# Two graph layers in one software pipeline: the second layer's mask moves from TensorE's products to GpSimd, with all lists and banks laid out anew

## The chip, the cores and the metric

The kernel runs on one core of a Trainium2 chip. The metric is the device time of one execution in microseconds, median of three runs. A core has TensorE (PE in the profile; PEld is its weight load), VectorE (DVE), ScalarE (ACT), GpSimd (POOL) and SyncE (SP), which here only issues DMAs. All share SBUF; PSUM has eight banks, each 128 partitions by 512 f32.

## The reference

64 graphs of 256 nodes with 256 features; `adj` has 0 and 1. Eight heads of width 32.

```
# layer 0
q, k = src@Wq+bq, src@Wk+bk;  attn = softmax(q k^T / sqrt(32))       # per head
out = sum over r of (attn * (adj == r)) @ (src@Wv[r] + bv[r])        # r = 0..3
x  = LN(src + out@Wo + bo);   x2 = LN(x + gelu(x@W1+b1)@W2 + b2)
# layer 1
e  = leaky_relu(q k^T, 0.2);  attn = softmax(where(adj > 0, e, -9e15))
h  = LN(attn @ v)
y  = LN(concat(h, x2) @ Wffn^T) + x2
```

Layer 0's softmax runs over all nodes, and the relations are sorted out afterwards; layer 1's runs over the neighbours alone, and it is this mask (`adj > 0`) that the change moves.

## The kernel before

One graph is worked on by four stages, and each engine's `body(g0, g1, g2, g3)` holds one period of its list: four neighbouring graphs, each in another stage, with g3 the youngest. `turns` runs the body 67 times: three partly filled at the start, a hardware loop, three partly empty at the end. The order of each list is written out by hand; semaphores (`sig`) tie them. Banks are assigned by number (`B_Q`, `B_RR`, ...), and many waits only say that a bank or a tile is free again.

Products that need f32 accuracy are made of three f32r products of high and low parts. So after most results comes a split: a cast to f32r (high part), then a subtraction (low part): `low` on GpSimd (L418, for act, att and xt) and `lo_part`, `biased_low` on VectorE (L719, L804). Scores are computed from stacks (`stack_a`, `stack_r`), in which SP's DMAs put high and low parts of one head under one another, three DMAs per pair of heads.

Per graph, on TensorE: stage g3 is layer 0's projections (`projection`, `vee`), score rows for the maxima (`score_rows`, L1103), their turning (`maxima_turned`), score columns (`score_cols`, L1112), and values (`both` for sums and relation 0, `one` for relation 1 minus 0, L1024). Stage g2 is out projection, FFN (`up`, `down`) and layer 1's projections. Stage g1 is layer 1's attention and FFN.

Layer 1's attention goes by four pairs of heads. `masked_rows(p, b)` (L1034 to L1041) writes 2 x 256 x 256 scores and adds `off_q` (bf16, 0 or -9e15) by an identity matrix; then ScalarE's `low` copies 0.2 times the scores to `leaky_s` (L534), VectorE's `leaky` takes the maximum of both (L790), `lowest_row` reduces the row maximum (L794), ScalarE's `exp_rows` (L540) applies exp in place with the row sums, TensorE's `turn` (L1048) transposes, ScalarE copies to `probs`, and `row_values` multiplies with v. `leaky_s` has three slots for four pairs.

GpSimd's other work: `masked(p)` (L424) multiplies layer 0's exp with `rel1` (adj == 1) in pairs of 128x512; `make_rstd` (L412, L414) for the four layer norms LN_A, LN_M (layer 0), LN_H, LN_O (layer 1); `residual` (L430). VectorE's `centre` (L740) and `rescale` (L746) are the norms' two passes, each in two halves. `rel1` is made on VectorE at L829, `off_q` at L850, and L856 checks adj_a. In the list before, GpSimd waits for LN_H's rescale before its second `masked`:

```
if g0 is not None:
    pool.wait_ge(ln_mv[LN_H].sem, ln_mv[LN_H].at(g0))
    make_rstd(LN_H, g0)
    pool.wait_ge(ln_done[LN_H].sem, ln_done[LN_H].at(g0))
```

Of the kernel before, what the change touches and what calls it, by code (L numbers as in the profile page):

```python
# [29 lines left out]
P = 128  # L30
# [78 lines left out]
def build(nc, x, xT, adj, adjT, w):  # L109
    ctx = ExitStack()  # L110
    with ctx:
# [32 lines left out]
        identb = sb("identb", [P, P], BF16)  # L144
# [55 lines left out]
        def bank(b):  # L200
            return pair[b // 2][:, b % 2]

        B_AO, B_ADEN, B_Q, B_K, B_WO, B_X1T, B_RV, B_HN = 2, 6, 7, 6, 1, 4, 4, 2
        B_DN, B_N1T, B_FFN, B_AMT, B_X2T, B_LQ, B_LK, B_LV = 1, 1, 3, 4, 1, 4, 7, 7
        B_X = 0
        B_V, B_UP = (5, 7), (4, 6, 1, 5)
        B_RR, B_TN, B_AR, B_AC = (0, 2, 1, 0), (0, 1, 1, 3), (3, 1, 2, 3), (2, 3, 2, 0)
# [31 lines left out]
                                                   sig("low_r_done", PAIRS))  # L239
        exp_r_done, turned_mm, probs_r = sig("exp_r_done", PAIRS), sig("turned_mm", PAIRS), sig("probs_r", PAIRS)  # L240
# [49 lines left out]
        def _(sp):  # L290
# [29 lines left out]
            def body(g0, g1, g2, g3):  # L320
                if g2 is not None:
                    load(xn, x, g2, "(t p) c -> p t c", ld_xn)
                if g3 is not None:
                    load(xt, xT, g3, "(t p) n -> p t n", ld_xt)
                if g2 is not None:
                    sp.wait_ge(ashift.sem, ashift.at(g2))
                    for s in range(2):
                        sp.dma_start(stack_a[STK + s:STK + s + 1, 0, :, :].bitcast(F32),
                                     shift_a[32 * s:32 * s + H, :].bitcast(F32)).then_inc(ashifted.sem, 16)
                    if path.general:  # L330
                        load_x_terms(g2)
                if g1 is not None:
# [4 lines left out]
                    stack(3, stack_r, stacked_r)  # L337
                if g2 is not None:
                    load(adj_q, adj, g2, "(t p) n -> p t n", ld_adj_r)
                if g3 is not None:  # L340
                    sp.wait_ge(qk_split.sem, qk_split.at(g3))
                    stack(0, stack_a, stacked_a)
                    stack(1, stack_a, stacked_a)
                    stack(2, stack_a, stacked_a)
                    stack(3, stack_a, stacked_a)
                    load(adj_a, adjT, g3, "(t p) n -> p t n", ld_adj_a)
                if g0 is not None:
                    sp.wait_ge(ln_done[LN_O].sem, ln_done[LN_O].at(g0))
                    sp.dma_start(out[g0 - path.general * G].rearrange("(t p) c -> p t c", p=P), result[:]).then_inc(stored.sem, 16)

# [46 lines left out]
        def _(pool):  # L397
# [28 lines left out]

            def residual():
# [18 lines left out]
            def body(g0, g1, g2, g3):  # L446
                if g1 is not None:
                    pool.wait_ge(att_hi_done.sem, att_hi_done.at(g1))
                    low(att_lo[:], att[:], att_hi[:]).then_inc(att_split.sem, 1)
                    pool.wait_ge(ln_mv[LN_A].sem, ln_mv[LN_A].at(g1))  # L450
                    make_rstd(LN_A, g1)
                    pool.wait_ge(act_hi_done.sem, act_hi_done.at(g1, 1))
                    low(act_lo[:, 0], act[:, 0], act_hi[:, 0]).then_inc(act_split.sem, 1)
                    pool.wait_ge(act_hi_done.sem, act_hi_done.at(g1, 2))
                    low(act_lo[:, 1], act[:, 1], act_hi[:, 1]).then_inc(act_split.sem, 1)
                    pool.wait_ge(act_hi_done.sem, act_hi_done.at(g1, 3))
                    low(act_lo[:, 2], act[:, 2], act_hi[:, 2]).then_inc(act_split.sem, 1)
                    pool.wait_ge(act_hi_done.sem, act_hi_done.at(g1))
                    low(act_lo[:, 0], act[:, 0], act_hi[:, 0]).then_inc(act_split.sem, 1)
# [3 lines left out]
                if g0 is not None:  # L463
                    pool.wait_ge(ln_done[LN_M].sem, ln_done[LN_M].at(g0))
                    if ran(g0, 1):
                        pool.wait_ge(ln_done[LN_O].sem, ln_done[LN_O].at(g0 - 1))
                    residual().then_inc(x2k_done.sem, 1)
                if g1 is not None:
                    pool.wait_ge(ln_mv[LN_M].sem, ln_mv[LN_M].at(g1))
                    make_rstd(LN_M, g1)  # L470
                if g2 is not None:
                    pool.wait_ge(probs_a.sem, probs_a.at(g2, 1))
                    pool.wait_ge(rel1_done.sem, rel1_done.at(g2))
                    masked(0).then_inc(probs1_done.sem, 1)
# [33 lines left out]
        def _(act_e):  # L508
# [862 lines left out]
```

## Time and profile before

| | before |
|---|---|
| time, median of 3 runs (lowest, highest) | 3195.21 us (3192.64, 3196.96) |
| the profiled execution's span | 3190.8 us |
| TensorE busy | 3103.2 us (97%) |
| VectorE busy | 2604.6 us (82%) |
| ScalarE busy | 2056.7 us (64%) |
| GpSimd busy | 1432.6 us (45%) |
| mean granted TensorE clock | 0.989 |

The profile gives the profiled execution's time as the span from its first to its last instruction; there is no other time of that execution. A steady period is one graph. TensorE's durations overlap each other, since a product starts before the last one has drained; its cost is read from the distance between starts. On VectorE, too, a next independent instruction starts about 0.09 us before the end of the last.

### The profile page before, as it was taken

Reading aid. Unit: us, or ns where it says so; the run is one execution under the profiler, and the core shown is the slowest. Engines: PE = TensorE matmul, PEld = TensorE weight load, DVE = VectorE, ACT = ScalarE, POOL = GpSimd, SP = SyncE. Lnnn points to the kernel's source line nnn. Section 1 sums busy time; section 2 is a strip of 40 time slices with the busy share of each in tenths; the row PEclk is TensorE's granted clock in tenths of the full one; section 3 lists DMA queues with packets and bytes.
Section 4 is the critical chain, followed back from the end, with each engine's and each line's share of the span. In section 5 each row is a group of like instructions: output and inputs, shape, how many; then the busy total and the mean of one; then the engine's idle time right before and its main releaser. Section 6 shows DMA issues by size and latency. Waiting matters only on the chain.

```text
span 3190.8 us, 76499 instructions
## 1 busy us (share of the span) xinstructions
PE 3103.2 (97%) x28139; PEld 2715.8 (85%) x28328; DVE 2604.6 (82%) x4896; ACT 2056.7 (64%) x4303; POOL 1432.6 (45%) x1549
## 2 busy tenths in 40 slices
PE   5999999999999999999999999999999999999996
PEld 4888888888888888888888888888888888888885
DVE  4788888888888888888888888888888888888884
ACT  2565766766766766766766766766766766666664
POOL 1445445445445445445445445445344444444441
PEclk8999999999999999999999999999999999999997
DMA  4343344344334334434434434433433433433431
GB/s 111 84 101 93 89 94 97 89 92 98 91 89 98 94 86 98 96 83 98 99 81 98 102 79 97 105 79 94 107 79 92 110 79 89 112 80 89 107 81 31
DMA packets 218074, 292.76 MB, mean 92 GB/s; under 512 B 31796, under 2 KB 119479, under 8 KB 218039
## 3 DMA queue, kind: packets, MB, share of 16 engines
q1 hardware_dynamic: 218038, 292.30, 39.0%
q8 instruction: 22, 0.36, 0.0%
q14 instruction: 14, 0.11, 0.0%
HBM read 73.02 MB, written 16.78 MB: 28 GB/s over the span
## 4 chain that ended last, share of the span: by engine, by line
PE 90%; ACT 3%; issue 3%; DVE 2%; SPq 1%; DMA 1%; POOL 0%; POOLq 0%; DVEq 0%; ACTq 0%
PE pair L994 50%; PE pair L1024 15%; PE pair L1048 7%; PE pair L1038 6%; PE pair L1103 4%; PE pair L1112 2%; PE pair L1040 2%; ACT probs L561 2%; PE pair L1012 2%; SPq L299 1%; PE pair L999 1%; PE pair L1119 0%; ACT leaky_s L540 0%; DMA stack_a<-qk 0%; DMA probs<-in_w 0%
## 5 line engine op out<-in xcount | busy, mean ns | idle before, releaser
L418 POOL TENSOR_TENSOR act_r_lo<-act,act_r_hi 128x512 fp32r<-128x512 f32 x256 | 335.3, 1319 | 741.6 <-DVE act_r_hi L931 537.5
L540 ACT ACTIVATE leaky_s<-leaky_s,low_r 128x256 f32<-128x256 f32 x1024 | 506.1, 499 | 2.7 <-DVE low_r L794 2.0
L424 POOL TENSOR_TENSOR probs<-probs,rel 128x512 f32<-128x512 f32 x256 | 293.4, 1168 | 207.0 <-ACT probs L561 119.8
L561 ACT ACTIVATE probs<-pair 128x1024 f32<-128x1024 f32 x256 | 256.8, 1029 | 189.9 <-PE pair L1112 189.9
L798 DVE TENSOR_REDUCE mx_a<-pair 128x4 f32<-128x1024 f32 x256 | 307.7, 1223 | 78.1 <-PE pair L1103 78.0
L534 ACT ACTIVATE leaky_s<-pair 128x1024 f32<-128x1024 f32 x256 | 262.6, 1026 | 158.7 <-PE pair L1040 158.7
L790 DVE TENSOR_TENSOR leaky_s<-pair,leaky_s 128x1024 f32<-128x1024 f32 x256 | 312.4, 1220 | 37.8 <-ACT leaky_s L534 37.5
L794 DVE TENSOR_REDUCE low_r<-leaky_s 128x4 f32<-128x1024 f32 x256 | 310.8, 1214 | 2.2
L530 ACT ACTIVATE probs<-pair 128x1024 f32<-128x1024 f32 x256 | 261.8, 1023 | 65.1 <-PE pair L1048 60.9
L424 POOL TENSOR_TENSOR leaky_s<-probs,rel 128x512 f32<-128x512 f32 x256 | 291.0, 1173 | 0.2 <-ACT probs L561 0.2
L1048 PE MATMUL pair<-ident,leaky_s 128*128 128x128 f32 x2048 | 269.7, 275 | 6.7 <-ACT leaky_s L540 5.8
L555 ACT ACTIVATE act<-pair,bias_col 128x256 f32<-128x256 f32 x512 | 215.8, 476 | 76.4 <-PE pair L994 75.0
L1048 PEld LDWEIGHTS pair<-ident,leaky_s 128*128 128x128 f32 x2048 | 237.0, 142 | 18.5 <-ACT leaky_s L540 7.5
L412 POOL TENSOR_TENSOR rstd<-mv,eps 128x2 f32<-128x2 f32 x256 | 73.0, 285 | 398.4 <-DVE mv L735 398.4
L1038 PE MATMUL pair<-stack_r 96*128 96x256 f32 x1024 | 242.3, 348 | 4.6 <-DMA stack_r<-qk 3.2
L874 DVE RECIPROCAL att<-pair 128x512 f32<-128x512 f32 x64 | 214.9, 3358 | 36.6 <-PE pair L1024 36.6
L1024 PE MATMUL pair<-probs,v_a 128*32 128x256 f32 x3072 | 207.0, 387 | 11.7 <-ACT probs L561 11.6
L1038 PEld LDWEIGHTS pair<-stack_r 96*128 96x128 f32 x1024 | 179.2, 194 | 42.2 <-issue 25.9
L994 PE MATMUL pair<-xt_r_hi,w_hi 128*128 128x256 f32 x1024 | 211.3, 287 | 1.4 <-DVE xt_r_lo L719 1.4
L530 ACT ACTIVATE v_r<-pair 128x512 f32<-128x512 f32 x64 | 38.2, 597 | 269.8 <-PE pair L994 269.8
L994 PE MATMUL pair<-w_hi,act_r_hi 128*128 128x256 f32 x1024 | 209.9, 286 | 0.0
L994 PE MATMUL pair<-xt_r_hi,w_lo 128*128 128x256 f32 x1024 | 206.2, 283 | 0.0
(193 smaller groups left out, 8839.7 us busy)
## 6 DMA issues: line engine op xcount, KB each, us to landing
stack_a<-qk SPq DMA_DIRECT2D x768, 128.0 KB, 2.5
stack_r<-qk SPq DMA_DIRECT2D x768, 128.0 KB, 2.4
xt<-in_xT SPq DMA_DIRECT2D x64, 256.0 KB, 3.4
adj_a<-in_adjT SPq DMA_DIRECT2D x64, 256.0 KB, 3.0
xn<-in_x SPq DMA_DIRECT2D x64, 256.0 KB, 3.2
adj_q<-in_adj SPq DMA_DIRECT2D x64, 256.0 KB, 2.9
out<-n SPq DMA_DIRECT2D x64, 256.0 KB, 2.8
probs<-in_w SPq DMA_DIRECT2D x4, 512.0 KB, 4.6
```

What stands on the lines that cost most here:

```text
L418: return nc.gpsimd.tensor_tensor(dst, src, hi, ALU.subtract)
L424: last = nc.gpsimd.tensor_tensor(masked_p[g][:, h], probs[:, g, h], rel1[:], ALU.mult)
L530: return nc.scalar.activation(dst, src, ACT.Copy)
L540: last = nc.scalar.activation(leaky_s[:, p % SLOTS, k, t], leaky_s[:, p % SLOTS, k, t], ACT.Exp, bias=low_r[:, p, k, t:t + 1], accum_out=d ...
L561: return nc.scalar.activation(probs[:, g, 2 * q:2 * q + 2], pair[b][:], ACT.Exp, scale=SCALE)
L790: return nc.vector.tensor_tensor(leaky_s[:, p % SLOTS], pair[b][:], leaky_s[:, p % SLOTS], ALU.max)
L794: return nc.vector.tensor_reduce(low_r[:, p], leaky_s[:, p % SLOTS], AX.X, ALU.max, negate=True)
L798: return nc.vector.tensor_reduce(mx_a[:, :, p * NG:(p + 1) * NG].rearrange("p t h -> p h t"), pair[b][:], AX.X, ALU.max)
L994: last = mm(dst, lhs(i, t), rhs(j, t), start=start and n == 0, stop=stop and n == len(steps) - 1, skip_group_check=skip)
L1024: last = mm(bank(b)[h * DH:(h + 1) * DH, g, :], v(t, g * GH + h), pr(h, t), start=first and t == 0, stop=stop and t == NT - 1, skip_group_ ...
L1038: mm(pair[b][:, k, t], stack_r[:, 0, slot(h), t * P:(t + 1) * P], stack_r[:, 1, slot(h), :], start=t == 0, stop=False, skip_group_check=True)
L1048: last = nc.tensor.transpose(pair[b][:, k, c, t * P:(t + 1) * P], leaky_s[:, p % SLOTS, k, t, c * P:(c + 1) * P], ident[:])
```

## The change

The mask of layer 1 goes. In its place GpSimd adds `off_q` in place to `leaky_s`, between `leaky` and `lowest_row`, under a new signal `masked_r`. `identb` and the identity products are gone. All five lists and all bank numbers are new, and with them the waits on banks. The core of it:

```diff
-        identb = sb("identb", [P, P], BF16)
-        B_AO, B_ADEN, B_Q, B_K, B_WO, B_X1T, B_RV, B_HN = 2, 6, 7, 6, 1, 4, 4, 2
-        B_DN, B_N1T, B_FFN, B_AMT, B_X2T, B_LQ, B_LK, B_LV = 1, 1, 3, 4, 1, 4, 7, 7
+        B_AO, B_ADEN, B_Q, B_K, B_WO, B_X1T, B_RV, B_HN = 3, 2, 4, 2, 3, 0, 3, 0
+        B_N1T, B_DN, B_FFN, B_AMT, B_X2T, B_LQ, B_LK, B_LV = 4, 0, 5, 1, 1, 7, 0, 5
-        B_V, B_UP = (5, 7), (4, 6, 1, 5)
-        B_RR, B_TN, B_AR, B_AC = (0, 2, 1, 0), (0, 1, 1, 3), (3, 1, 2, 3), (2, 3, 2, 0)
+        B_V, B_UP = (3, 1), (1, 7, 0, 1)
+        B_RR, B_TN, B_AR, B_AC = (3, 0, 3, 1), (2, 2, 3, 1), (1, 3, 2, 1), (3, 0, 1, 3)
+        masked_r = sig("masked_r", PAIRS)
...
+            def without_edges(p):
+                for k in range(2):
+                    last = nc.gpsimd.tensor_tensor(leaky_s[:, p % SLOTS, k], leaky_s[:, p % SLOTS, k], off_q[:], ALU.add)
+                return last
...
-            def masked_rows(p, b):
+            def second_rows(p, b):
                 for k, h in enumerate((p, p + GH)):
                     for t in range(NT):
-                        mm(pair[b][:, k, t], stack_r[:, 0, slot(h), t * P:(t + 1) * P], stack_r[:, 1, slot(h), :],
-                           start=t == 0, stop=False, skip_group_check=True)
-                    last = mm(pair[b][:, k], identb[:], off_q[:], start=False, stop=True, skip_group_check=True)
+                        last = mm(pair[b][:, k, t], stack_r[:, 0, slot(h), t * P:(t + 1) * P], stack_r[:, 1, slot(h), :],
+                                  start=t == 0, stop=True, skip_group_check=True)
```

The new lists, one period each, in words ("A(g3)" is A for the youngest graph; waits for data left out):

- SP: xt(g3); the shift's two DMAs(g2); adj_a(g3), which waits for the check of the graph before; stack_r 0, 1, 2(g1); adj_q(g2); stack_r 3(g1); stack_a 1, 0, 2, 3(g3); store(g0); xn(g3). Before, xn and xt stood first, adj_q behind stack_r 3, and adj_a behind stack_a, in the order 0, 1, 2, 3.
- GpSimd: low part of xt(g3), low part of att(g2), edges 0, edges 1(g1), rstd LN_A(g2), rstd LN_O(g0), edges 2, edges 3(g1), low part of act 0(g2), residual(g1), low parts of act 1, 2, 3(g2), rstd LN_M(g2), masked 0, 1(g3), rstd LN_H(g1), masked 2, 3(g3). "Edges" is `without_edges`.
- ScalarE: exp_cols 0, 1, 2(g2), x2t(g1), exp_cols 3(g2), the two copies of layer 1's q and k(g1), n1t(g0), low 0, 1, 2(g1), biased q, k(g3), v_r(g1), exp_rows 0(g1), v_a 0, 1(g3), x1t(g2), exp_rows 1, low 3, copy of turned 0(g1), gelu 0, 1, 2(g2), copy 1(g1), gelu 3(g2), exp_rows 2, 3, copies 2, 3, copy of the values(g1).
- VectorE: cast of xt(g3); reciprocal, minimum of the check, attention multiply, cast of att(g2); LN_O statistics(g0); leaky 0(g1); LN_O centre(g0); leaky 1(g1); residual and LN_A statistics(g2); lowest_row 0(g1); LN_A centre(g2); biased_low q(g3); LN_A rescale(g2); lowest_row 1(g1); biased_low k(g3); low part of x1t(g2); leaky 2(g1); LN_O rescale(g0); leaky 3, lowest_row 2(g1); cast of act 0(g2); rel1(g3); cast of act 1(g2); lowest_row 3(g1); cast of act 2(g2); maxima 0 to 3(g3); cast of act 3(g2); shift(g3); rden(g1); residual, LN_M statistics, centre, rescale, off_q(g2); per_head(g1); low part of x2t(g2); LN_H statistics, centre, rescale(g1); check of adj_a(g3); qk_lo 0, 1(g2); low part of n1t(g1).
- TensorE: wq(g3), rows 1(g1), out projection(g2), rows 2(g1), wk(g3), lv(g1), vee 0, 1(g3), x1t(g2), turn 0, rows 3(g1), up 0, 1, 2(g2), turn 1(g1), up 3(g2), score_rows 0, 1, 2(g3), down 0(g2), score_rows 3(g3), down 1(g2), turn 2(g1), turned maxima(g3), down 2(g2), turn 3(g1), down 3(g2), row values(g1), score_cols 0, 1(g3), FFN's x2t half(g1), score_cols 2(g3), turned values(g1), x2t(g2), score_cols 3, both 0(g3), lq, lk(g2), n1t(g1), both 1(g3), FFN's other half(g1), one 0, 1(g3), rows 0(g2). "Rows" is `second_rows`. Before, lv stood behind the FFN's half, and turn 1 before up 0.

## Rows read from the trace of the kernel before

**Rows 1.** The page: span; busy time of each engine, share, instructions.
```profile
span 3190.8 us, 76499 instructions
PE 3103.2 (97%) x28139; PEld 2715.8 (85%) x28328; DVE 2604.6 (82%) x4896; ACT 2056.7 (64%) x4303; POOL 1432.6 (45%) x1549
```
**Rows 2.** The page: the chain that ended last, by engine.
```profile
PE 90%; ACT 3%; issue 3%; DVE 2%; SPq 1%; DMA 1%; POOL 0%; POOLq 0%; DVEq 0%; ACTq 0%
```
**Rows 3.** VectorE's line 874: durations in ns, first and last start in us.
```profile
L874 DVE RECIPROCAL att<-pair x64: 3357/3358/3359, 68.4 to 3096.7; 128x512 f32<-128x512 f32 x64
```
**Rows 4.** One steady period: length; busy PE, PEld, DVE, ACT, POOL; clock, DMA, GB/s.
```profile
1502.30:1550.39 48.09, 47.92 (x439) 42.10 (x443) 40.28 (x77) 31.94 (x68) 22.34 (x25) 1.00 0.40 93
```
**Rows 5.** Timeline of TensorE, merged: start, us to the last one's end.
```profile
1518.43 0.87 PE L1038 MATMUL pair<-stack_r 96*128 96x256 f32 x4
...
1519.61 0.41 PE L994 MATMUL pair<-wo_lo,att_r_hi 128*128 128x256 f32 x2
...
1528.87 0.40 PE L994 MATMUL pair<-xt_r_lo,w_hi 128*128 128x256 f32 x2
...
1538.90 0.71 PE L1103 MATMUL pair<-stack_a 96*128 96x256 f32 x4
1539.44 0.40 PE L994 MATMUL pair<-w_hi,act_r_hi 128*128 128x256 f32 x2
...
1541.74 0.38 PE L1119 MATMUL pair<-ident,mx_a 128*8 128x128 f32 x2
...
1546.21 0.50 PE L994 MATMUL pair<-wf_hi,x2t_hi 128*128 128x256 f32 x2
```
**Rows 6.** Timeline of GpSimd: four mask multiplies in a row.
```profile
1508.66 4.54 POOL L424 TENSOR_TENSOR leaky_s<-probs,rel 128x512 f32<-128x512 f32 x4
```
**Rows 7.** Timeline of VectorE in the same period.
```profile
1510.14 3.36 DVE L874 RECIPROCAL att<-pair 128x512 f32<-128x512 f32 x1 [0.41 <-PE pair L1024]
...
1516.41 0.68 DVE L886 TENSOR_TENSOR att<-pair,att 128x512 f32<-128x512 f32 x1
1517.13 0.43 DVE L888 CAST att_r_hi<-att 128x512 fp32r<-128x512 f32 x1
1517.47 1.21 DVE L794 TENSOR_REDUCE low_r<-leaky_s 128x4 f32<-128x1024 f32 x1
1518.60 1.22 DVE L790 TENSOR_TENSOR leaky_s<-pair,leaky_s 128x1024 f32<-128x1024 f32 x1
...
1522.03 0.75 DVE L731 BATCH_NORM_STATS2 stats<-res 128x6 f32<-128x256 f32 x2
...
1523.04 0.84 DVE L804 SCALAR_TENSOR_TENSOR qk<-pair,bias_col,qk 128x256 fp32r<-128x256 f32 x2
1523.80 0.87 DVE L740 SCALAR_TENSOR_TENSOR x<-res,mv,norm 128x256 f32<-128x256 f32 x2
```
**Rows 8.** Timeline early on: VectorE's check, the GpSimd multiplies; the check's group.
```profile
106.39 1.65 DVE L856 SCALAR_TENSOR_TENSOR adj_a<-adj_a,rel 128x512 int32<-128x512 int32 x1
...
106.14 1.35 POOL L424 TENSOR_TENSOR probs<-probs,rel 128x512 f32<-128x512 f32 x1
...
107.45 1.62 POOL L424 TENSOR_TENSOR leaky_s<-probs,rel 128x512 f32<-128x512 f32 x1
...
L856 DVE SCALAR_TENSOR_TENSOR adj_a<-adj_a,rel 128x512 int32<-128x512 int32 x64 | 45.4, 709 | 0.0
```
**Rows 9.** Timeline: a cast of act beside GpSimd's subtraction.
```profile
1533.57 0.61 DVE L937 CAST act_r_hi<-act 128x512 fp32r<-128x512 f32 x1
...
1532.60 1.29 POOL L418 TENSOR_TENSOR act_r_lo<-act,act_r_hi 128x512 fp32r<-128x512 f32 x1 [8.43 <-DVE act_r_hi L931]
```
**Rows 10.** Waits of GpSimd: in total, times, longest.
```profile
POOL probs L424 <- DVE n L746: 87.2, 62, 1.4
```
**Rows 11.** While draining: a gap of TensorE, then the clock (columns as rows 4).
```profile
3111.49 0.66 PE L1012 MATMUL pair<-ident,x 128*128 128x128 f32 x4 [2.12 <-DVE x L746]
...
3112.90:3116.20 3.30, 3.30 (x18) 3.30 (x18) 2.62 (x3) 2.31 (x2) 0.00 (x0) 0.53 0.00 0
```

More of the change, by code:

```diff
@@ L446, in body @@
             def body(g0, g1, g2, g3):
[L447 to L459, printed above, removed]
                 if g3 is not None:
@@ L854, in body @@
-                if g2 is not None and not path.general:
-                    dve.wait_ge(rel1_done.sem, rel1_done.at(g2))
-                    nc.vector.scalar_tensor_tensor(adj_a[:], adj_a[:], 0, rel1[:], ALU.is_equal, ALU.add,
-                                                   accum_out=known[:]).then_inc(known_done.sem, 1)
-                if g0 is not None:
-                    dve.wait_ge(ln_mid[LN_H].sem, ln_mid[LN_H].at(g0))
-                    dve.wait_ge(ln_rstd[LN_H].sem, ln_rstd[LN_H].at(g0))
-                    rescale(LN_H, n1, row(LB1))
@@ L901, in body @@
                     statistics(LN_A, res, g2)
+                if g1 is not None:
+                    dve.wait_ge(masked_r.sem, masked_r.at(g1, 1))
+                    lowest_row(0).then_inc(low_r_done.sem, 1)
+                if g2 is not None:
+                    dve.wait_ge(ln_mv[LN_A].sem, ln_mv[LN_A].at(g2))
+                    centre(LN_A, res, G1, x1)
                 if g3 is not None:
@@ new lines, in body @@
+                if g2 is not None:
+                    dve.wait_ge(down_mm.sem, down_mm.at(g2))
+                    nc.vector.tensor_tensor(res[:], bank(B_DN), x1[:], ALU.add).then_inc(res_m_done.sem, 1)
+                    dve.wait_ge(res_m_done.sem, res_m_done.at(g2))
+                    statistics(LN_M, res, g2)
+                    dve.wait_ge(ln_mv[LN_M].sem, ln_mv[LN_M].at(g2))
+                    centre(LN_M, res, G2, x2)
+                    dve.wait_ge(ln_mid[LN_M].sem, ln_mid[LN_M].at(g2))
+                    dve.wait_ge(ln_rstd[LN_M].sem, ln_rstd[LN_M].at(g2))
+                    rescale(LN_M, x2, row(E2))
+                    dve.wait_ge(ld_adj_r.sem, ld_adj_r.at(g2))
+                    nc.vector.tensor_scalar(off_q[:], adj_q[:], 0, NEG, ALU.is_le, ALU.mult).then_inc(off_done.sem, 1)
@@ new lines, in body @@
+                if g1 is not None:
+                    dve.wait_ge(heads_r.sem, heads_r.at(g1))
+                    statistics(LN_H, n1, g1)
+                    dve.wait_ge(ln_mv[LN_H].sem, ln_mv[LN_H].at(g1))
+                    centre(LN_H, n1, LG1, n1)
+                    dve.wait_ge(ln_mid[LN_H].sem, ln_mid[LN_H].at(g1))
+                    dve.wait_ge(ln_rstd[LN_H].sem, ln_rstd[LN_H].at(g1))
+                    rescale(LN_H, n1, row(LB1))
+                if g3 is not None and not path.general:
+                    nc.vector.scalar_tensor_tensor(adj_a[:], adj_a[:], 0, rel1[:], ALU.is_equal, ALU.add,
+                                                   accum_out=known[:]).then_inc(known_done.sem, 1)
```

444 lines of the change are left out of this document (221 added, 223 removed).

## The prediction

> **What bounds the kernel now.** The page comes first. TensorE is busy for 97% of the span, VectorE for 82%, ScalarE for 64% and GpSimd for 45% [rows 1], and the chain that ended last lies on TensorE for 90% [rows 2]. In steady state, VectorE's reciprocal, one per graph, has its first start at 68.4 us and its last at 3096.7 [rows 3]: 3028.3 us for 63 periods. A single period in the middle is 48.09 us with TensorE busy for 47.92 at full clock [rows 4], so 0.17 us of it is idle. The rest of the span, 68.4 + 94.1 = 162.5 us, is filling and draining.
>
> All sums are made against the span of 3190.8 us. The median of the timed runs is 3195.2, so 4.4 us is added at the end.
>
> **What TensorE is rid of.** Eight identity products per graph go. Durations of products overlap, so I take distances. A layer-2 block runs from 1518.43 to the output projection's real start: its second pair stands at 1519.61 and pairs stand 0.24 apart, so 1519.37: 0.94 us. The same four products without a mask, layer 1's score rows, take 1538.90 to 1539.44: 0.54 [rows 5]. So a block loses 0.40 us here; where the score rows follow products of full width they take 0.47, and beside the value products a masked block took over 1.0, so up to 0.55. Four blocks: 2.0 us per graph (bounds 1.6 and 2.3). TensorE's floor becomes 48.09 - 0.17 - 2.0 = 45.9 us. Whether TensorE gets down to it, the other engines decide.
>
> **What GpSimd gets.** Eight adds of 128x512 f32 with bf16. The nearest row is the mask multiply of the same shape and types: four of them in 4.54 us, 1.14 each from start to start [rows 6]. So 2.3 us per pair, 9.1 per graph; GpSimd goes from 22.3 [rows 4] to 31.5 us per period. Each add also lengthens the way leaky, reduce, exp, turn by 2.3 us plus two semaphores.
>
> **The new lists, uncontended.** I walk one period by the new order, with VectorE's starts in a row from [rows 7], a semaphore at 0.05 to 0.1 us. t = 0 is the end of layer 1's last value products (`one(1)`). VectorE has to do, with nothing between: attention multiply 0.72, its cast 0.34, LN_O statistics 1.01, leaky(0) 1.13, centre 0.79, leaky(1) 1.13, residual 0.73, LN_A statistics 1.01, lowest_row(0) 1.13, centre 0.79, biased_low 0.76, rescale 0.80, lowest_row(1) 1.13, biased_low 0.76, x1t's low part 0.69 = 12.92 us. It starts at t = 0.2, since the reciprocal (3.36 long, started 0.1 after `both(1)`) ends 3.45 after `both(1)` and the value products 3.39. So up(0) can start at 13.2. TensorE's own work up to there (wq, wk, lv 1.43 each, two vee 1.5 each, out projection 1.66, x1t 0.36, one turn 0.9, four score blocks 2.1) is 12.4. So 0.8 us of the 2.0 is lost to VectorE: it is late next. From up(0) (its second pair stands at 1528.87, so 1528.6) to the end of the next `both(1)` (0.1 before the reciprocal, 1510.14 + 48.09) TensorE took 29.4 before [rows 5, 7]; with turn(1) moved in (0.93) and without the 0.17 us wait, 30.2. Period: 3.6 + 13.0 + 30.2 = 46.8 us, 81 us less in 63 periods.
>
> **What this walk leaves out: GpSimd and VectorE hold each other up.** The trace shows it where GpSimd's multiplies follow one another early on: VectorE's check of adj_a, two SBUF tensors in, takes 1.65 us instead of 0.71 on average, and ends at 108.04, which is 0.55 after the end (107.49) of the GpSimd instruction that began 0.25 before it; the next GpSimd multiply then takes 1.62 instead of 1.14 [rows 6, 8]. In steady state the cast of act_hi that starts in the middle of a GpSimd subtraction ends at 1534.18, 0.29 after that subtraction's end (1533.89), and takes 0.61 us; with the pair free such a cast takes 0.43 [rows 7, 9]. Reductions, PSUM reads and leaky (one SBUF tensor) keep their duration. And the kernel before holds the multiplies back until LN_H's rescale is over: GpSimd idles 1.4 us per graph there [rows 10]. The new list has no such wait.
> The Trainium skill (SBUF — State Buffer, the section Who interferes with whom) says the same as a rule: VectorE in a 2-port mode or with two SBUF inputs, and GpSimd, hold that pair exclusively, and the other one fully blocks. The trace agrees as far as these rows go (0.29 and 0.55 us after release).
>
> I take it that the two alternate, in order of arrival: VectorE ends 0.28 after GpSimd's end, the next GpSimd instruction 1.05 to 1.14 after VectorE's. Then two stretches are redone.
>
> *From x1t's low part (13.1) to the last maximum.* leaky(2) ends 14.26, and GpSimd starts edges(2) beside LN_O's rescale (n and x2k, both in SBUF): its first half ends 14.65, the first add 15.7, the second half 16.0, the second add 17.1. leaky(3) starts 15.9 (uncontended 14.96) and ends 17.1; edges(3) then starts. lowest_row(2) 17.2 to 18.3; the cast of act_hi(0) waits for the first add of edges(3): 18.7; the second add ends 19.75; rel1 (newly placed here) 20.0; act_lo(0) 21.2; the cast of act_hi(1) 21.5; lowest_row(3) 22.6; the cast of act_hi(2) waits for x2k: 23.0; four maxima (1.13 each) end 27.6. That is 14.5 us after 13.1. Uncontended TensorE would be at the turned maxima at 25.7, so it loses 2.0 (bounds 0.3, only the casts' 0.19 each, and 2.5). Behind the first maximum waits score_rows(3), behind the last one all of down(2), turn(3), down(3), row values.
>
> *From there to layer 1's first exp* TensorE runs: turned maxima, turn(3), down(3) and row values, 1541.74 to 1546.21 before [rows 5], and now down(2) (1.44) and score_cols(0) (0.5) too: 6.4 us. With exp's 1.03 and two semaphores: 7.6.
>
> *From exp(0) to the reciprocal* (s = 0 is the end of exp(0)). GpSimd: multiply 1.5 (it waits for LN_M's second rescale), off_q's cast between, multiplies 2.9, 4.0, 5.1; rstd of LN_H 6.4, where LN_H's centre got in at 5.1 and 5.4. Multiplies 5 and 6 now meet LN_H's rescale, 7 and 8 the check of adj_a: rescale's halves end 7.1 and 8.3 (uncontended 6.8), multiply 6 at 9.4, the check 9.9, multiplies 7 and 8 11.0 and 12.1, the cast of xt_hi 12.3, the reciprocal starts 12.4. qk_lo's two parts and n1t's low part (about 0.65 each) come behind the check and end at 11.9, so the second half of the FFN, uncontended in place at 9.9, waits too. This costs 2.0 on TensorE and 0.35 more on the multiply at t = 0 (bounds 0 and 3.2, the latter if GpSimd gets the pair first at LN_H's rescale).
>
> The closed chain: reciprocal to attention multiply 3.45, to x1t's low part 12.92, to the last maximum 14.5, to exp(0) 7.6, to the reciprocal 12.4 = **50.9 us per graph**, 2.8 more than now.
>
> **Filling and draining.** Without the overlap of graphs the adds lie on the path: about one pair, 2.4 us, in the last body, and stack(1) now goes ahead of stack(0), 6 issues and not 3 before the first score rows (0.65 each): 2 us. The identity products saved there are worth 2. I take +4 (bounds -3 and +12): 166.5.
>
> **Sum.** 166.5 + 63 x 50.9 = 3373; with 4.4: **3378 us**, 5.7% slower.
>
> The loads moved in SP's queue cost nothing here: adj_a's now waits for the check, over at s = 9.9, and is issued (0.5) before the layer-2 split at 11.2; adj_q goes ahead of stack(3) and puts its landing at t = 6.0, behind which ScalarE's bias of q waits (3.1 later than before), but VectorE needs that only at t = 9. The xn load is a period early. ScalarE has 32 us in 51 and is late nowhere by more than 0.3. The banks laid out anew put waits where their release is over 0.4 us before; only qk_split before score block 3 binds (12.5 against 12.05), inside the 0.8.
>
> **Rivals.**
> 1. *The two do not block each other as I say*: GpSimd's instructions give way, or starts fall beside each other, so that the casts cost 0.19 us more and no more. For it: LN_A's centre at 1523.80 keeps its 0.87 us per pair beside one of GpSimd's small instructions [rows 7]. Against: [rows 8]. Then 46.8 us, 166.5 + 2948.4 + 4.4 = 3119 us, faster. It decides from 1.3 us of blocking on the path per graph; I count 4.1. Chance 0.25.
> 2. *TensorE stays full*: VectorE's 12.92 us are partly run ahead. 45.9 x 63 + 162.5 + 4.4 = 3059. Against: `one(1)` gates the multiply, and in the new list VectorE has nothing left to do ahead of it. 0.03.
> 3. *Blocking in one of the two stretches only* (2.0): 48.9 us, 3252, slower. 0.2; a share of it, 0.04, lands within 0.2% of now.
> 4. *TensorE's clock falls in the new gaps.* Draining, soon after a gap of 2.12 us, the granted clock was 0.53 for 3.3 us, its lower level [rows 11], which costs 1.5. Once per graph: 52.4 us, 3473. In steady state it was 1.00 with no gaps to test it; the new gaps are 0.8 to 1.4 us. 0.1.
> My forecast, with what lies around it (49.5 to 51.7 us per graph): 0.42.
>
> **How the numbers follow.** A difference under 0.2% (6 us) is taken as none. Faster: rivals 1 and 2, 0.28. Same 0.04. Slower 0.68. The range reaches from rival 1 to beyond the forecast: 3115 to 3430; below it are rival 2 and half of rival 1, above it rival 4. The forecast's own range is 3290 to 3430.
>
> **What would show it.** Right: reciprocals 50 to 52 us apart; TensorE idle 4 to 6 us per graph, released by VectorE (maxima, LN_H's rescale, n1t's low part); act_hi casts, off_q, xt_hi, rescale well above their durations before, some over 1 us; GpSimd's adds near 1.17. Wrong: TensorE busy over 97% with reciprocals under 47.5 apart; rescale of LN_O and LN_H still 0.48 although an add or multiply runs beside them. The step most likely to be off is the order of arrival at LN_O's and LN_H's rescale.

## The result, and the profile after

The changed kernel takes 3371.9 us (median of 4, 3369.3 to 3372.6) beside 3193.9 for the kernel before on the same chip: ratio 1.0555, 95% interval 1.054 to 1.057. It is 5.6% slower; the forecast was 3378 us.

The page of the kernel after, as [rows 1, 2]: the span, the engines, the chain by engine.
```profile
span 3369.7 us, 75854 instructions
...
PE 3025.3 (90%) x27816; PEld 2633.2 (78%) x27816; DVE 2979.8 (88%) x4895; ACT 2047.8 (61%) x4303; POOL 2130.3 (63%) x2061
...
DVE 22%; ACT 21%; POOL 16%; PE 13%; issue 13%; SPq 10%; DMA 4%; DVEq 0%; POOLq 0%; ACTq 0%
```
TensorE has 78 us less to do and is no longer full: 90% and not 97%, and its share of the chain falls from 90 to 13%, the rest being spread over every engine. VectorE has one instruction fewer than before and is busy for 375 us more: its instructions have grown longer.

The reciprocal, as [rows 3]:
```profile
L834 DVE RECIPROCAL att<-pair x64: 3341/3344/3358, 67.6 to 3274.5; 128x512 f32<-128x512 f32 x64
```
One steady period, with the columns of [rows 4]:
```profile
1643.96:1694.98 51.02, 46.78 (x435) 40.80 (x435) 46.39 (x77) 31.71 (x67) 33.40 (x32) 1.00 0.37 88
```
So 3206.9 us for 63 periods, 50.90 each, and 162.8 around them. TensorE is idle for 4.2 us per period, at full clock all the same. What it waits for (us in total, times, longest):
```profile
PE pair L1024 <- DVE n L757: 87.9, 63, 4.1
PE pair L1114 <- DVE mx_a L809: 74.2, 62, 1.4
PE pair L1006 <- DVE att_r_lo L730: 55.7, 64, 1.4
PE pair L1130 <- DVE mx_a L809: 28.6, 60, 7.5
PE pair L1050 <- DVE qk L815: 22.2, 60, 0.4
```
These are the turn of n1 behind LN_H's rescale (1.4 us per graph), score_rows(3) and the turned maxima behind the maxima (1.2 and 0.4), the second half of the FFN behind n1t's low part (0.9) and score block 3 behind k's low part (0.36).

VectorE's instructions on SBUF, grouped by line and shape (busy us, mean ns of one):
```profile
L757 DVE SCALAR_TENSOR_TENSOR n<-n,rstd,norm 128x256 f32<-128x256 f32 x128 | 163.1, 1313 | 40.6 <-POOL rstd L418 40.6
L757 DVE SCALAR_TENSOR_TENSOR n<-n,rstd,x2k 128x256 f32<-128x256 f32 x128 | 113.6, 928 | 0.2 <-POOL rstd L418 0.2
L966 DVE SCALAR_TENSOR_TENSOR adj_a<-adj_a,rel 128x512 int32<-128x512 int32 x64 | 104.0, 1626 | 0.0
L904 DVE CAST act_r_hi<-act 128x512 fp32r<-128x512 f32 x64 | 95.0, 1484 | 0.7 <-ACT act L572 0.7
L947 DVE TENSOR_SCALAR off_q<-adj_q 128x512 bf16<-128x512 int32 x64 | 88.4, 1382 | 0.0
L901 DVE TENSOR_SCALAR rel<-adj_a 128x512 bf16<-128x512 int32 x64 | 80.3, 1255 | 0.0
```
From the top: LN_H's rescale, LN_O's rescale, the check of adj_a, the cast of act 1, off_q, rel1. The same in the kernel before, where the check took 709 ns [rows 8]:
```profile
L746 DVE SCALAR_TENSOR_TENSOR n<-n,rstd,norm 128x256 f32<-128x256 f32 x128 | 55.8, 475 | 0.3 <-POOL rstd L414 0.3
L746 DVE SCALAR_TENSOR_TENSOR n<-n,rstd,x2k 128x256 f32<-128x256 f32 x128 | 55.8, 478 | 0.3 <-POOL rstd L414 0.3
L937 DVE CAST act_r_hi<-act 128x512 fp32r<-128x512 f32 x64 | 39.2, 613 | 1.0 <-ACT act L555 1.0
L850 DVE TENSOR_SCALAR off_q<-adj_q 128x512 bf16<-128x512 int32 x64 | 27.7, 433 | 0.0
L829 DVE TENSOR_SCALAR rel<-adj_a 128x512 bf16<-128x512 int32 x64 | 34.4, 537 | 0.0
```
The instructions are the same; what runs on GpSimd beside them is new. Two stretches of the timeline show it, VectorE first and GpSimd's rows for the same time behind:
```profile
1661.35 1.79 DVE L757 SCALAR_TENSOR_TENSOR n<-n,rstd,x2k 128x256 f32<-128x256 f32 x2
...
1665.78 1.40 DVE L901 TENSOR_SCALAR rel<-adj_a 128x512 bf16<-128x512 int32 x1
1667.10 1.52 DVE L904 CAST act_r_hi<-act 128x512 fp32r<-128x512 f32 x1
...
1688.74 2.61 DVE L757 SCALAR_TENSOR_TENSOR n<-n,rstd,norm 128x256 f32<-128x256 f32 x2 [0.65 <-POOL rstd L418]
1691.27 1.65 DVE L966 SCALAR_TENSOR_TENSOR adj_a<-adj_a,rel 128x512 int32<-128x512 int32 x1
...
1661.51 2.66 POOL L434 TENSOR_TENSOR leaky_s<-leaky_s,off_q 128x512 f32<-128x512 f32 x2 [4.20 <-DVE leaky_s L801]
1664.35 2.54 POOL L434 TENSOR_TENSOR leaky_s<-leaky_s,off_q 128x512 f32<-128x512 f32 x2 [0.18 <-DVE leaky_s L801]
1666.85 1.48 POOL L422 TENSOR_TENSOR act_r_lo<-act,act_r_hi 128x512 fp32r<-128x512 f32 x1
...
1688.61 5.33 POOL L428 TENSOR_TENSOR leaky_s<-probs,rel 128x512 f32<-128x512 f32 x4
```
rel1 ends at 1667.18, 0.29 after the second add of the last pair (1666.89); the cast of act 1 at 1668.62, 0.29 after act_lo's first subtraction (1668.33). At 1688.61 GpSimd starts its fifth multiply 0.13 ahead of LN_H's rescale, and the durations of both halves of the rescale and of the check add up to 4.3 us where they were 1.7; the four multiplies beside them take 5.33, not 4.54 [rows 6].

### The profile page after: what moved, and what is told of

The parts are those of the page before. It is cut to its first block, busy times and chain, and to the rows that moved or that the text cites. A ratio compares the mean times of both kernels' runs of the same rounds, so it can differ in the third digit from the quotient of the medians.

```text
span 3369.7 us, 75854 instructions
## 1 busy us (share of the span) xinstructions
PE 3025.3 (90%) x27816; PEld 2633.2 (78%) x27816; DVE 2979.8 (88%) x4895; ACT 2047.8 (61%) x4303; POOL 2130.3 (63%) x2061
## 4 chain that ended last, share of the span: by engine, by line
DVE 22%; ACT 21%; POOL 16%; PE 13%; issue 13%; SPq 10%; DMA 4%; DVEq 0%; POOLq 0%; ACTq 0%
SPq L299 9%; PE pair L1006 9%; POOL probs L428 8%; ACT leaky_s L557 8%; DVE mx_a L809 7%; DMA stack_r<-qk 4%; POOL leaky_s L428 3%; POOL rstd L418 3%; ACT L572 2%; ACT qk L565 2%; DVE n L757 2%; DVE rel L901 2%; PE pair L1059 2%; DVE adj_a L966 2%; ACT v_a L547 2%
## 5 line engine op out<-in xcount | busy, mean ns | idle before, releaser
L434 POOL TENSOR_TENSOR leaky_s<-leaky_s,off_q 128x512 f32<-128x512 f32 x512 | 618.1, 1232 | 345.4 <-DVE leaky_s L801 345.3
L422 POOL TENSOR_TENSOR act_r_lo<-act,act_r_hi 128x512 fp32r<-128x512 f32 x256 | 348.4, 1371 | 173.3 <-DVE act_r_hi L929 163.1
L428 POOL TENSOR_TENSOR probs<-probs,rel 128x512 f32<-128x512 f32 x256 | 311.5, 1248 | 88.8 <-ACT probs L578 88.8
L428 POOL TENSOR_TENSOR leaky_s<-probs,rel 128x512 f32<-128x512 f32 x256 | 340.0, 1357 | 0.0
L809 DVE TENSOR_REDUCE mx_a<-pair 128x4 f32<-128x1024 f32 x256 | 294.9, 1210 | 0.4 <-PE pair L1114 0.3
L416 POOL TENSOR_TENSOR rstd<-mv,eps 128x2 f32<-128x2 f32 x256 | 61.2, 239 | 309.1 <-DVE mv L746 308.9
L572 ACT ACTIVATE act<-pair,bias_col 128x256 f32<-128x256 f32 x512 | 201.3, 480 | 41.2 <-POOL act_r_lo L422 37.3
L1114 PE MATMUL pair<-stack_a 96*128 96x256 f32 x1024 | 151.5, 291 | 79.7 <-DVE mx_a L809 74.2
L422 POOL TENSOR_TENSOR att_r_lo<-att,att_r_hi 128x512 fp32r<-128x512 f32 x64 | 82.1, 1283 | 208.5 <-DVE att_r_hi L843 208.5
L418 POOL TENSOR_TENSOR rstd<-rstd,power 128x2 f32<-128x2 f32 x256 | 197.9, 773 | 20.0
```

Source lines behind the costliest of these rows:

```text
L418: nc.gpsimd.tensor_tensor(rstd[:, k, 1, :], rstd[:, k, 0, :], power[:], ALU.pow).then_inc(ln_rstd[k].sem, 1)
L422: return nc.gpsimd.tensor_tensor(dst, src, hi, ALU.subtract)
L428: last = nc.gpsimd.tensor_tensor(masked_p[g][:, h], probs[:, g, h], rel1[:], ALU.mult)
L434: last = nc.gpsimd.tensor_tensor(leaky_s[:, p % SLOTS, k], leaky_s[:, p % SLOTS, k], off_q[:], ALU.add)
L809: return nc.vector.tensor_reduce(mx_a[:, :, p * NG:(p + 1) * NG].rearrange("p t h -> p h t"), pair[b][:], AX.X, ALU.max)
```

## The experiments

A table first, which the verdicts rest on. "After" is the changed kernel; all others are edits of it, but for e6, an edit of the kernel before. Period and the distances from one reciprocal's start are in us, medians over periods in the middle of each run. "x1t" is the end of x1t's low part, "maxima" the end of the last maximum, "heads" the start of per_head, "n1t" the end of n1t's low part. The ratio is to the kernel before, with its 95% interval.

| kernel | us | ratio | period | x1t | maxima | heads | n1t |
|---|---|---|---|---|---|---|---|
| after | 3371.9 | 1.0555 (1.054-1.057) | 50.96 | 16.34 | 30.70 | 40.28 | 50.70 |
| e1 GpSimd waits for LN_H | 3222.7 | 1.0084 (1.007-1.010) | 48.55 | 16.34 | 30.70 | 40.28 | 48.01 |
| e2 rel1 early | 3321.2 | 1.0393 (1.038-1.041) | 50.14 | 16.34 | 29.49 | 39.47 | 49.88 |
| e3 no adds | 3308.5 | 1.0357 (1.034-1.037) | 49.94 | 16.34 | 29.70 | 39.27 | 49.69 |
| e4 writes only | 3324.6 | 1.0402 (1.039-1.042) | 50.23 | 16.34 | 29.95 | 39.57 | 49.98 |
| e5 identity products back | 3372.5 | 1.0551 (1.053-1.057) | 51.01 | 17.22 | 30.76 | 40.34 | 50.76 |
| e6 before, no wait | 3224.8 | 1.0087 (1.007-1.010) | 48.53 | | | | |
| e7 e1 and e2 | 3173.6 | 0.9927 (0.991-0.994) | 47.77 | 16.35 | 29.48 | 39.50 | 47.22 |
| e8 e7, more moved | 3212.3 | 1.0048 (1.003-1.007) | 48.47 | 16.35 | 29.49 | 39.50 | 47.20 |
| e10 e8, cast of xt early | 3164.3 | 0.9903 (0.989-0.992) | 47.65 | 16.37 | 29.51 | 39.53 | 47.24 |
| e11 e7, cast of xt early | 3163.9 | 0.9902 (0.989-0.992) | 47.63 | 16.37 | 29.51 | 39.51 | 47.25 |
| e12 e7, wait for LN_O too | 3198.1 | 1.0012 (1.000-1.002) | 48.17 | 16.34 | 29.91 | 39.90 | 47.63 |
| e13 e7, identity products | 3217.3 | 1.0060 (1.005-1.007) | 48.50 | 17.22 | 30.65 | 40.23 | 47.95 |

**e1: one wait back.** In GpSimd's list, ahead of the third pair of multiplies:
```
+                if g1 is not None:
+                    pool.wait_ge(ln_done[LN_H].sem, ln_done[LN_H].at(g1))
                 if g3 is not None:
                     pool.wait_ge(probs_a.sem, probs_a.at(g3, 3))
                     masked(2)
```


> The changed kernel, with one wait added: GpSimd starts masked(2) only after LN_H's rescale. Theory 1 (GpSimd and VectorE exclude each other): rescale's two halves fall from 2.61 to 0.87 us, TensorE no longer waits 1.35 for n1 nor 0.86 for n1t's low part, the period falls from 50.96 to 48.8 us: 163 + 63 x 48.8 + 2 = 3239 us (3220 to 3290). Theory 2 (the adds have made GpSimd's list and the way through it longer, and the order of the lists does the rest): a wait more on GpSimd can only make masked(2) and masked(3) later: 3372 or slower.

3222.7, at the quick end of the range. LN_H's rescale and the check in the groups, and GpSimd's wait:
```profile
L759 DVE SCALAR_TENSOR_TENSOR n<-n,rstd,norm 128x256 f32<-128x256 f32 x128 | 56.3, 481 | 40.5 <-POOL rstd L418 40.5
L968 DVE SCALAR_TENSOR_TENSOR adj_a<-adj_a,rel 128x512 int32<-128x512 int32 x64 | 44.6, 696 | 0.0
```
```profile
POOL leaky_s L428 <- DVE n L759: 70.6, 62, 1.1
```
GpSimd now idles 1.1 us per graph, as it did in the kernel before (1.4, [rows 10]), and the period shrinks by 2.41: everything up to per_head stands where it stood (40.28), and n1t's low part ends 2.69 earlier (0.28 of it goes to the cast of xt, now beside a multiply: 690 ns, not 410). TensorE's waits for n and n1t's low part are gone, those for the maxima stay (74.0 and 26.4). This one wait takes back 149 of the 178 us lost.

**e2: rel1 ahead of leaky(2)**, so that neither it nor the act casts behind it meet the adds.
```
+                    nc.vector.tensor_scalar(rel1[:], adj_a[:], 1, None, ALU.is_equal).then_inc(rel1_done.sem, 1)
                     leaky(2, B_RR[2]).then_inc(leaky_done.sem, 1)
```


> The changed kernel, with rel1 (tensor_scalar of adj_a) moved on VectorE from between the casts of act 0 and act 1 to ahead of leaky(2), where GpSimd is idle. Theory 1: rel1 takes 0.43 and not 1.40 us, the cast of act 1 0.5 to 1.5; the maxima come 1.1 us earlier, period 49.9, 3309 us (3290 to 3345). Theory 2: the same VectorE work in the same stretch, no change, 3372.

3321.2, inside. The maxima end 1.21 earlier, the period shrinks by 0.82; the difference is a new wait, the first line here:
```profile
PE pair L1006 <- POOL act_r_lo L422: 38.2, 63, 1.1
```
Down(1) waits 0.6 us for act_lo's second chunk, which GpSimd, busy with adds and x2k, gives late.

**e3, e4, e5: what is it in the adds?** e3 leaves the mask out, and the adds with it; e4 leaves it out too and has a memset of the block in each add's place (`nc.gpsimd.memset(leaky_s[:, p % SLOTS, k].bitcast(BF16), 0.0)`), GpSimd writing and reading nothing, behind an add of two elements per partition; e5 is e3 with the mask put back on TensorE:
```
+                    last = mm(pair[b][:, k], identb[:], off_q[:], start=False, stop=True, skip_group_check=True)
```


> The changed kernel without GpSimd's adds: layer 1's mask is left out altogether, lowest_row waits for leaky alone (and two waits order the rescale of LN_O against x2k). Theory 1: of the 4.1 us of blocking only about 1.6 of the 2.0 in the stretch with the adds goes; act_lo against the casts and the multiplies against LN_H, the check and off_q stay: period 49.6, 3287 us (3265 to 3310), still slower than before although TensorE does 2 us less per graph. Theory 2 (the adds themselves, their 9 us and the longer way): TensorE's or VectorE's floor, 45.9 to 46.8 us, 3055 to 3115.

> The changed kernel with each pair's two adds replaced by a two-element add and two memsets of leaky_s (1024 bf16 elements each), so that GpSimd is busy at the same place but reads no large tile; layer 1's scores are zeroed by it. If a memset takes about 1.05 us, GpSimd's time stays near 2.3 us per pair. Theory 1 as the page on SBUF words it (two-input VectorE instructions are held up by GpSimd's reads only, 2-port ones by its writes too): LN_O's rescale falls from 0.9 to 0.48 us per half, the casts stay held up; period 50.2, 3328 us (3300 to 3355). Theory 1 with any GpSimd instruction blocking: 3372. Theory 2: 3372 by equal time, less only by as much as the memsets are shorter.

> The changed kernel's lists and banks, with layer 1's mask given back to TensorE's identity products and no adds on GpSimd. Theory 1: the run without adds and without mask has a period of 49.94 us; TensorE's 2.0 us more lie mostly in the stretch up to up(0), where it had 0.8 free and 0.6 comes back at the maxima: 50.5, 3345 us (3310 to 3360). LN_H's rescale stays at 1.31 per half. Theory 2 (putting the mask on GpSimd is what costs): about the kernel before, 3195.

e3: 3308.5, inside; e4: 3324.6, near its middle; e5: 3372.5, 12 us beyond its range. The adds cost 1.02 us per period, all of it between x1t and the maxima (30.70 against 29.70). LN_O's rescale in e4, and the memset:
```profile
L763 DVE SCALAR_TENSOR_TENSOR n<-n,rstd,x2k 128x256 f32<-128x256 f32 x128 | 55.7, 476 | 0.2 <-POOL rstd L419 0.2
...
L436 POOL MEMSET leaky_s<- 128x1024 bf16 x512 | 470.8, 951 | 0.0
```
In e4 a memset begins 0.08 us into the rescale's second half, and both halves take 0.48 us (476 ns is their mean). In the changed kernel an add stands there, and the second half takes 1.40 us (the first keeps 0.48; 928 ns is the mean of both). So here an instruction of VectorE with two tensors in SBUF is held up by what GpSimd reads, not by what it writes. Without the reading, 0.73 of the adds' 1.02 us are gone (a part of that because a memset is also 0.2 us shorter than an add). A cast is held up by writing too: act 0's, which starts 0.53 into a memset, takes 0.69 and ends 0.28 after it.
The Trainium skill (SBUF — State Buffer, Who interferes with whom) states this split: a VectorE instruction with two SBUF inputs contends with a GpSimd instruction that reads SBUF and not with one that only writes it; one in a 2-port mode, which a cast can enter, contends with GpSimd either way. The trace agrees: the rescale's second half takes 0.48 us beside the memset and 1.40 beside the add, and the cast is held up by a memset too.

e5's miss is mine: I took it that TensorE's extra work would hide in its waits. TensorE is busy for 48.21 us in a period of e5 and for 46.79 in one of e3, and of the difference 0.88 us comes at once: x1t's low part ends at 17.22, not 16.34, since score blocks 0 to 2 lie on the way to it. (These 1.4 us of busy time are less than the products cost; see e13, and step 1 of the section on why the prediction was right.) TensorE's idle time in e3 lies behind that point, but for 0.36 us ahead of score block 3 and 0.08 ahead of the out projection. And blocking that has nothing to do with the mask (LN_H's rescale stays at 1312 ns) keeps e5 5.5% above the kernel before.

**e6: the kernel before without its wait** for LN_H's rescale.
```
                     make_rstd(LN_H, g0)
-                    pool.wait_ge(ln_done[LN_H].sem, ln_done[LN_H].at(g0))
```


> The kernel before, with one wait taken out: GpSimd no longer waits for LN_H's rescale before masked(1). Nothing else is changed. Theory 1: the multiply starts 1.4 us earlier, beside the check and the rescale; rescale's halves end 1.8 us later, n1's transposes are late by 0.5, period 48.6 instead of 48.09: 3229 us (3205 to 3260). Theory 2: the wait was idle time of an engine with 55% to spare, 3194 or a little less.

3224.8, near what was expected. The rescale takes 1356 ns there, 1.75 us more for its two halves, but the turn of n1 waits only 26.4 us in all (0.4 per graph) and the period grows by 0.5. The check stands ahead of the rescale in that list and is not held up (724 ns, 709 before). So the old list had slack behind the rescale; in the new one, where the check is held up too, the blocking costs 2.4.

**e7: both.** e1's and e2's edits together.

> The changed kernel with both of the first two edits: the wait for LN_H's rescale ahead of masked(2), and rel1 ahead of leaky(2). Theory 1: the two stretches are independent, so the gains add: 50.96 - 2.40 - 0.88 = 47.7 us per graph, 3170 us (3150 to 3200), faster than before.

3173.6, within 4 us of what was expected, and 0.7% faster than the kernel before. The two gains add up (2.41 + 0.82 against 3.19). TensorE's waits are down to three of weight:
```profile
PE pair L1008 <- POOL act_r_lo L422: 39.1, 64, 1.2
PE pair L1052 <- DVE qk L817: 21.6, 59, 0.4
...
PE pair L1052 <- DMA stack_r<-qk: 7.7, 7, 1.8
```

**e8: everything that meets GpSimd moved away**: off_q and the check into VectorE's idle 2.6 us ahead of LN_M's residual, x2k behind act_lo's third chunk.

> As the one with both edits, and off_q and the check of adj_a moved on VectorE into its idle stretch before LN_M's residual (2.57 us per graph), and GpSimd's residual moved behind the low part of act 2, where GpSimd idles. Theory 1: the cast of act 2, the cast of xt and off_q are no longer held up; near VectorE's floor of 46.8: 47.2 us per graph, 3138 us (3115 to 3165). If the check of adj_a, off_q and x2k were not on the path, 3170 as the run before it.

3212.3, slower than e7 and 47 us beyond the range: a clear miss. Up to n1t's low part nothing changed (table). Behind it stands the cast of xt beside the multiplies, in e8 and then in e7:
```profile
1614.48 1.43 DVE L832 CAST xt_r_hi<-xt 128x512 fp32r<-128x512 f32 x1
...
1612.21 4.72 POOL L428 TENSOR_TENSOR leaky_s<-probs,rel 128x512 f32<-128x512 f32 x4 [1.14 <-DVE n L760]
```
```profile
1593.66 0.71 DVE L831 CAST xt_r_hi<-xt 128x512 fp32r<-128x512 f32 x1
...
1591.49 3.89 POOL L428 TENSOR_TENSOR leaky_s<-probs,rel 128x512 f32<-128x512 f32 x3 [1.15 <-DVE n L759]
```
Off_q had stood ahead of a wait of VectorE for per_head's input and the check ahead of one for ScalarE's part of k; without them VectorE idles there (1.47 and 0.62 us), so nothing was gained. But in e7 the check had started ahead of the first multiply, which waited for it and took 1.47 us (1591.49 to 1592.96); the cast of xt then came 0.42 before the end of the second (1594.08) and took 0.71. In e8 the first takes 1.16, the second ends at 1614.50, the third starts at 1614.46, and the cast comes at 1614.48, 0.02 us behind it: it waits the third out and takes 1.43, with the reciprocal right behind. That is the whole of the 0.70 us lost per period.
TensorE's wait for act_lo is gone, and in its place the next turn waits 0.73 us for exp, at the same distance from the reciprocal (29.1): ScalarE was as late as GpSimd.

**e10, e11: the cast of xt moved** a body ahead, into the same idle stretch, in e8 and in e7. VectorE's hardware loop ends one body earlier for it, since the last graph has no successor whose xt could be cast.
```
+                if g3 is not None and not path.general and not last_xt(g3):
+                    if g2 is None:
+                        dve.wait_ge(v_mm.sem, v_mm.at(g3))
+                    dve.wait_ge(ld_xt.sem, ld_xt.at(g3 + 1))
+                    nc.vector.tensor_copy(xt_hi[:], xt[:]).then_inc(xt_hi_done.sem, 1)
                 if g2 is not None:
                     dve.wait_ge(down_mm.sem, down_mm.at(g2))
```


> e8's lists, and the cast of xt_hi for the next graph moved out of the stretch before the reciprocal into VectorE's idle stretch ahead of LN_M's residual. Theory: e8 lost nothing but one cast. Between e7 and e8 every event up to per_head stands at the same distance from the reciprocal (33.1 us to the turn and 39.5 to per_head within 0.05), off_q's and the check's time turned into waits for exp and for ScalarE's part of qk (1.5 and 0.6 us idle), and the cast of xt_hi took 1.43 us instead of 0.71, because the check no longer held the multiplies up. Then this kernel's period is 48.43 less 0.7 less the part of the cast that stood between the value products' end and the reciprocal (0 to 0.2): 47.6, a time of 3162 us (3150 to 3178), and TensorE's waits for att's low part are gone. Rival (GpSimd's late residual and the moved check cost something themselves): 3195 to 3212, near e8.

> e7's lists with only the cast of xt_hi moved into VectorE's idle stretch. In e7 layer 1's last value products end 0.2 us before the reciprocal starts; 0.1 of that is the semaphore, so the cast can give back 0.1 us per graph and no more, although it is 0.63 long: TensorE is then late next. 3165 us (3155 to 3174). Rival (VectorE's row of work before the reciprocal is still the bound, the cast's whole 0.63 come back): 3134.

3164.3 and 3163.9, both within 3 us of what was expected, and the rival's 3134 is refuted. So e8's loss was the cast; and taking 0.63 us off VectorE in e7 gives back 0.14 per period, since layer 1's last value products end just ahead of the reciprocal. These two are the fastest kernels here, 1.0% below the kernel before.

**e12: the same wait for LN_O** (`pool.wait_ge(ln_done[LN_O].sem, ...)` ahead of the third pair of adds), on e7.

> e7 with GpSimd waiting for LN_O's rescale before the third pair of adds. Theory: the wait takes 0.85 us off the rescale (0.93 to 0.48 per half) and 0.8 off the start of leaky(3), but GpSimd has no idle time between its third pair of adds and act_lo's third chunk, so it starts the pair 0.85 later and makes it up only by the 0.4 to 0.7 us that it is itself held up in the two pairs; act_lo's second chunk, for which TensorE waits 0.6 us, moves by -0.1 to +0.3. 3180 us (3165 to 3200): a wait that was worth 2.4 us per graph at LN_H is worth nothing at LN_O. Rival (every such wait gains, because the blocking costs more than it): 3130 to 3150.

3198.1, at the slow end of the range. The rescale is not held up (477 ns), and GpSimd makes up the 0.86 us by which it starts later: its four adds take 4.54 without a break, and end 23.29 us after the reciprocal, against 23.21.
```profile
1575.67 4.54 POOL L434 TENSOR_TENSOR leaky_s<-leaky_s,off_q 128x512 f32<-128x512 f32 x4 [5.41 <-DVE n L761]
...
1578.00 1.22 DVE L809 TENSOR_REDUCE low_r<-leaky_s 128x4 f32<-128x1024 f32 x1 [1.35 <-POOL leaky_s L434]
1579.14 1.36 DVE L905 CAST act_r_hi<-act 128x512 fp32r<-128x512 f32 x1
```
What I had left out: VectorE's lowest_row(2) waits 1.35 us for the later pair, and the act cast behind it runs into the fourth add. This moves the blocking rather than ending it: the period grows by 0.4.

**e13: the move of the mask by itself**: e7's lists with the identity products of e5.

> e7's lists (GpSimd's wait for LN_H's rescale, rel1 ahead of leaky(2)), but the mask is added on TensorE by identity products again and GpSimd adds nothing. It says what the move of the mask is worth by itself once the lists don't hold VectorE up. TensorE was busy for 48.21 us in a period of e5 and for 46.79 in one of e3, so the eight products cost 1.4 us of it per graph, not the 2.0 that was predicted. Theory: with the wait back TensorE is late next all along, as in the kernel before: period 48.2 busy plus 0.1 to 0.3 idle = 48.4, time 3213 us (3200 to 3228), 1.2% above e7, and TensorE's waits for n and att_r_lo gone. Rival (the adds on GpSimd cost in e7 what the products cost here): 3173 to 3185. Rival (the new lists are worse than the old in themselves): above 3228.

3217.3, 4 us above what was expected. Against e7 at the same lists, adding the mask on GpSimd gains 0.73 us per graph, 1.3% (ratios to before 1.0060 and 0.9927). What the products cost TensorE can be read at score block 2, where it waits for nothing in either run. From the block's first start to the second pair of the products behind it, first in e13, then in e7:
```profile
1528.09 0.40 PE L1047 MATMUL pair<-stack_r 96*128 96x256 f32 x2
1528.33 0.39 PE L1049 MATMUL pair<-off_q,identb 128*128 128x512 bf16 x1
1528.37 0.59 PE L1047 MATMUL pair<-stack_r 96*128 96x256 f32 x2
1528.81 0.39 PE L1049 MATMUL pair<-off_q,identb 128*128 128x512 bf16 x1
1528.85 0.59 PE L1003 MATMUL pair<-xt_r_hi,wk_hi 128*128 128x256 f32 x2
1529.27 0.40 PE L1003 MATMUL pair<-xt_r_lo,wk_hi 128*128 128x256 f32 x2
```
```profile
1506.52 0.64 PE L1052 MATMUL pair<-stack_r 96*128 96x256 f32 x4
1507.00 0.40 PE L1008 MATMUL pair<-xt_r_hi,wk_hi 128*128 128x256 f32 x2
1507.24 0.40 PE L1008 MATMUL pair<-xt_r_lo,wk_hi 128*128 128x256 f32 x2
```
That is 1.18 and 0.72 us, so two identity products take 0.46 to 0.47; blocks 0 and 3 give the same. Four blocks: 1.9 us per graph. Of these e7 gets 0.73. TensorE idles 1.07 us per period in e7, above all 0.60 for act_lo and 0.35 for k's low part, and 0.50 in e13; the rest lies in the busy time (step 1 below).

## Why the prediction was right, by its own steps

The size and the cause were as forecast; the time was 6 us lower, which is the fixed part (3.7) and the distance from span to median (2.2 us, not 4.4). Segment by segment, predicted and measured in the period at 1643.96: reciprocal to attention multiply 3.45 and 3.44, to x1t's low part 12.92 and 12.90, to the last maximum 14.5 and 14.42, to exp(0) 7.6 and 7.75, to the reciprocal 12.4 and 12.51; sum 50.9 and 51.02 (mean period 50.90). The fixed part is 162.8, not 166.5: filling and draining cost nothing beyond before. One sum was off by 0.1: from 1528.63 to 1558.13 are 29.5 us and not 29.4, so the uncontended period is 46.9; the closed chain of 50.9 doesn't use it.

1. *TensorE's saving* was sized right: 2.0 us per graph forecast, 1.9 by the distances in e13 and e7. Busy time shows only 1.4 (48.21 in e5, 46.79 in e3). It understates the saving: a product that is last before a wait counts with its whole 0.28 us and not with the 0.12 to the next start, and without the mask TensorE waits more often. That VectorE's row of work sets the end of that stretch, as I had named it, is also borne out: on the period the saving was worth 1.07 (e3 against e5; forecast 1.2).
2. *The adds*, 2.3 us per pair: 4.54 for four in e12, where nothing holds them up; 1232 ns on average in the changed kernel, where some are held up.
3. *GpSimd and VectorE alternate, in order of arrival.* Shown: e1 takes off 2.41 us per graph, e2 0.82, e7 3.19; e3 shows that 1.02 of the loss in the first stretch goes with the adds. I had put 2.0 and 2.35 into the two stretches. The second is confirmed. Of the first, 1.2 is taken off the maxima in e7 with the adds in place: they end 13.1 us behind x1t's low part, where I had 12.5 uncontended and 14.5 contended; GpSimd's late act_lo keeps 0.4 of it from the period.
4. *At LN_H* the order of arrival was not the one in the sum but the one that I gave as the bound: GpSimd is 0.13 us ahead, both halves of the rescale are held up (2.61 us together), and the check too (1.65). In return the multiplies are over before the cast of xt, which keeps 0.41 us; I had charged it. From the end of exp(0), the rescale ends at 8.9 us where I had 8.3, and the last multiply at 11.5 where I had 12.1. That the stretch's length came out within 0.1 us (12.51 against 12.4) is partly luck: two misses of opposite sign, each about 0.6 us.
5. *Rivals.* "They don't block each other", given 0.25, is refuted by e1. Rival 2, TensorE full, is refuted by its 4.2 us of idle time per period. "One stretch only" is refuted by e1 and e2, each of which gains. "The clock falls" is refuted by the period's row: 1.00 with gaps of up to 1.35 us.

An account of the 2.87 us per graph between before (48.09) and after: new lists with both remedies and the mask still on TensorE +0.4 (e13), the mask moved -0.7 (e7), rel1 where the adds run +0.8 (e2), no wait at LN_H +2.4 (e1). Of that 0.4, about 0.3 is waiting: TensorE idles 0.50 us per period in e13 and 0.17 before, ahead of score_rows(3) and the turned maxima, for the maxima. Which change of the lists makes the maxima late stays open; no run takes it apart.

## What to carry to other kernels

An instruction moved to GpSimd is paid for on VectorE too: here in the rescales and the check, which read two SBUF tensors, and in the casts and rel1, when they ran beside it. Write down for each stretch which of the two arrives first, and what waits behind the loser. A wait on GpSimd that looks like lost time can be what protects a critical VectorE instruction: it was worth 2.4 us of 51 where GpSimd had time to spare (e1), and cost 0.4 where VectorE then had to wait for the adds (e12). And moving a harmless instruction away can lay the next one open (e8): ask what it was shielding. Where the order is decided by 0.02 or 0.13 us, as here, it has to be forced, or moved clear of the collision.

## What the hardware showed that I hadn't expected

- A GpSimd instruction that only writes doesn't touch VectorE's rescale (476 ns beside memsets of 951) but holds up a cast (0.69 us, ending 0.28 after the memset).
- The same blocking, 1.7 to 1.75 us on the two halves of LN_H's rescale, cost 2.4 us per graph in one list (the check held up with it) and 0.5 in the other.
- Who starts first decides how much is held up, and the period repeats it in every graph. At LN_H, GpSimd starts 0.13 us ahead, and the rescale's two halves take 2.61 us (1313 ns on average over 128 halves); at LN_O, VectorE starts 0.16 ahead, and they take 1.79 (928 ns on average).
